# A two-stage attention kernel: block 0 and the scores of block 1 on scaled fp16 parts, the first loads on three queues, and new hand-written orders

## The chip, the core and the metric

The kernel runs on one core of one Trainium2 chip. A core has TensorE (PE, matrix products; its weight loads are shown as PEld), VectorE (DVE), ScalarE (ACT), GpSimd (POOL), SyncE (SP), and 16 DMA engines that serve the queues on which SP, ACT and POOL issue transfers. The metric is the device time of one execution in microseconds (us).

## What is computed

Four images of 256 channels x 1024 points. Block 0 is a group norm, then softmax attention over the points with a residual. Block 1 takes its result x and adds a channel attention and a position attention, both with a residual, which gives 2x + beta * (channel attention) + alpha * (position attention).

```python
def _L0_conv_ref(x, ...):
    h = group_norm(x, gn_w, gn_b)                       # 32 groups
    q, k, v = conv1x1(h, wq, bq), conv1x1(h, wk, bk), conv1x1(h, wv, bv)
    w = softmax(einsum('bcq,bck->bqk', q, k) / sqrt(C))
    return x + conv1x1(einsum('bqk,bck->bcq', w, v), wo, bo)
def _L1_conv_ref(x, ...):
    att = einsum('bcn,bdn->bcd', x, x)                  # 256 x 256
    feat_e = einsum('bcd,bdn->bcn', softmax(max(att) - att), x)
    fb, fc, fd = conv1x1(x, wb, bb), conv1x1(x, wc, bc), conv1x1(x, wd, bd)   # 32, 32, 256 channels
    feat_p = einsum('bcm,bnm->bcn', fd, softmax(einsum('bkn,bkm->bnm', fb, fc)))
    return (beta * feat_e + x) + (alpha * feat_p + x)
```

## The kernel before

**Parts.** Every large product is made from a high and a low part of each operand: `product` (L872 to L875) issues three matmuls, high x high, high x low and low x high. Before the change the parts of block 0 are 32-bit (`f32r`, shown as f32 or fp32r): the weights `a_w` (wq and wk multiplied together) and `b_w` (wv and wo), the normalised input `xn_h` and `xn_l`, and `g_h` and `g_l`. The score operands of block 1, `fb_parts` and `fc_parts`, hold their high and low parts as 96 rows in f32r, so that one matmul makes all three terms. The softmax weights (`pieces`, landed as `land`), V, FD, ET and x1 are already scaled to fp16 parts.

**Steps.** PE works through a hand-written list, `PE_ORDER`; a step has a kind, an image and a number. G.b.c is A times xn for half of the points (12 matmuls of 512 columns), V.b.u is B times xn for four tiles of 128 points (24 matmuls of 256 columns), S0.b.j is one tile of 128 x 1024 scores of block 0 (12 matmuls of 512), S2.b.j the same of block 1 (2 matmuls of 512), O0 and O2 are the weighted sums (each unit x1 is 6 matmuls of 512; O2 has two more units for ET). FBC, FD, ATT, AT and ET belong to block 1. There are 32 S0 tiles, 32 S2 tiles, 8 G and 8 V.

**What follows a tile.** DVE takes its row maximum (max, L690), ACT the exponential (exp, L422), DVE a reciprocal (r, L702 and L704), ACT the high piece (a, L431), DVE the low piece (b, L550), and SP issues a DMA transpose into `land`. Three PSUM buffers hold all score-type results in turn (`SLOTS = 3`): a step that enters a buffer waits until the last user of it is done. `exps` and `pieces` are double. ACT, DVE, POOL and SP have order lists of their own; nothing is reordered at run time, so an instruction that waits holds up all behind it on its engine.

**The start.** SP loads image 0 and then, in its queue, gn_w, gn_b, wo, wv, wd and the small vectors, and then images 1 and 2; ACT loads wk, bq and wq. DVE takes image 0's statistics (bn.0, L726), PE averages them over groups (MEAN.0, VAR.0, L881), POOL makes the inverse root (rstd, L358), DVE the gain and shift (st1) and xn (x0n, L587), ACT its high part (x0h, L408), and DVE or POOL its low part (x0l). PE meanwhile makes bq's bias (BG, L893), the transpose of wo (WO, L900), A and B (L886), the rest of the weights (W) and column sums of absolute weights (SV), from which `fixed_scales` (lS, L612 on) takes the scales of the fp16 parts. G.0.0 and then S0.0.0 are the first large products.

## Time and profile before

| what | us |
|---|---|
| median of three runs (range) | 421.03 (420.3 to 421.5) |
| the profiled execution, its own time | 419.87 |
| the profiled execution, span from first to last instruction | 418.1 |
| PE busy | 399.9 (96%) |
| DVE busy | 307.5 (74%) |
| ACT busy | 240.4 (57%) |
| granted TensorE clock, mean | 0.998 |

The profile page gives the busy time of each engine, the span in 40 slices, and the costliest groups of instructions. A matmul's row gives its start and a modelled duration which overlaps the next one's, so what one matmul costs in a row of them is the distance between starts, not its duration.

### The profile page before, as it was taken

To read this page: it belongs to the slowest core of one execution; us is meant where nothing else is said; L and a number is where in the kernel's file an instruction comes from. 1 tells how busy PE (TensorE), PEld (TensorE's weight loads), DVE (VectorE), ACT (ScalarE), POOL (GpSimd) and SP (SyncE) were. 2 spreads that over 40 slices of the span, in tenths; PEclk is the share of its full clock that TensorE was granted. 3 is DMA by queue.
4 is the path that set the end of the run, shared out by engine and by line. 5 is a ranking of instruction groups with operands and counts; after the bars stand their busy time and mean duration, and the time that the engine had idled before them with its cause. 6 is when DMAs were issued, how large, how long until landed. Compare 5 with 4: busy or idle time off the path is not lost.

```text
span 418.1 us, 5612 instructions
## 1 busy us (share of the span) xinstructions
PE 399.9 (96%) x2012; PEld 253.9 (61%) x2012; DVE 307.5 (74%) x564; ACT 240.4 (57%) x314; POOL 47.5 (11%) x47
## 2 busy tenths in 40 slices
...
GB/s 229 261 45 19 119 114 96 89 68 186 17 100 122 78 88 118 101 120 157 103 88 114 51 102 125 151 102 50 163 140 57 134 88 152 104 195 124 167 192 51
DMA packets 155739, 47.89 MB, mean 115 GB/s; under 512 B 152320, under 2 KB 153664, under 8 KB 155712
## 3 DMA queue, kind: packets, MB, share of 16 engines
...
## 4 chain that ended last, share of the span: by engine, by line
PE 86%; DVE 7%; SPq 2%; issue 2%; DMA 1%; ACT 1%; POOL 0%; DVEq 0%; ACTq 0%
PE sum_ps L873 14%; PE sum_ps L875 14%; PE sum_ps L874 14%; PE score_ps L873 12%; PE score_ps L875 12%; PE score_ps L874 12%; PE score_ps L997 4%; PE score_ps L1018 3%; DVE pieces L550 1%; DMA x<-in_x_dram 1%; DVE bn_raw L726 1%; PE score_ps L1027 1%; DVE x L852 1%; SPq L292 1%; SPq L278 1%
## 5 line engine op out<-in xcount | busy, mean ns | idle before, releaser
L550 DVE SCALAR_TENSOR_TENSOR pieces<-exps,recip,pieces 128x1024 f16<-128x1024 f32 x64 | 88.6, 1388 | 19.9 <-ACT pieces L431 19.5
L431 ACT ACTIVATE pieces<-exps,recip 128x1024 f16<-128x1024 f32 x64 | 72.9, 1143 | 37.6 <-DVE recip L704 27.6
L690 DVE TENSOR_REDUCE negmax<-score_ps 128x1 f32<-128x1024 f32 x64 | 77.4, 1215 | 10.8 <-PE score_ps L997 5.3
L422 ACT ACTIVATE exps<-score_ps,negmax 128x1024 f32<-128x1024 f32 x32 | 35.6, 1112 | 38.1 <-DVE negmax L690 31.7
L873 PE MATMUL score_ps<-xn_h,g_h 128*128 128x512 f32 x128 | 52.8, 412 | 1.1 <-DVE g_l L547 1.1
L422 ACT ACTIVATE exps<-score_ps,negmax_s,scales 128x1024 f32<-128x1024 f32 x32 | 38.4, 1201 | 24.2 <-DVE negmax_s L694 13.8
L875 PE MATMUL score_ps<-xn_h,g_l 128*128 128x512 f32 x128 | 50.1, 391 | 0.0
L874 PE MATMUL score_ps<-xn_l,g_h 128*128 128x512 f32 x128 | 49.9, 390 | 0.0
L873 PE MATMUL sum_ps<-land,fd_h 128*128 128x512 f16 x128 | 48.8, 381 | 0.0
L873 PE MATMUL sum_ps<-land,v_h 128*128 128x512 f16 x128 | 48.7, 381 | 0.0
L874 PE MATMUL sum_ps<-land,fd_h 128*128 128x512 f16 x128 | 48.5, 379 | 0.0
L875 PE MATMUL sum_ps<-land,fd_l 128*128 128x512 f16 x128 | 48.5, 379 | 0.0
L874 PE MATMUL sum_ps<-land,v_h 128*128 128x512 f16 x128 | 48.5, 379 | 0.0
L875 PE MATMUL sum_ps<-land,v_l 128*128 128x512 f16 x128 | 48.5, 379 | 0.0
L378 POOL TENSOR_TENSOR x_parts<-x,x_parts 128x1024 f16<-128x1024 f32 x7 | 15.9, 2272 | 138.3 <-ACT x_parts L395 138.3
L364 POOL TENSOR_TENSOR xn_l<-xn,xn_h 128x1024 fp32r<-128x1024 f32 x6 | 15.5, 2600 | 131.9 <-ACT xn_h L408 87.0
L873 PEld LDWEIGHTS score_ps<-xn_h,g_h 128*128 128x128 f32 x128 | 24.1, 188 | 7.2 <-DVE g_l L547 1.2
L875 PEld LDWEIGHTS score_ps<-xn_h,g_l 128*128 128x128 f32 x128 | 24.0, 188 | 5.3
L874 PEld LDWEIGHTS score_ps<-xn_l,g_h 128*128 128x128 f32 x128 | 24.1, 188 | 4.9
L997 PE MATMUL score_ps<-fc_parts,fb_parts 96*128 96x512 f32 x64 | 24.5, 465 | 0.0
L859 DVE SCALAR_TENSOR_TENSOR x<-sum_ps,scales,x 128x512 f32<-128x512 f32 x16 | 11.3, 745 | 17.2 <-PE sum_ps L875 17.2
L873 PEld LDWEIGHTS sum_ps<-land,fd_h 128*128 128x128 f16 x128 | 12.5, 98 | 17.7 <-issue 5.2
...
## 6 DMA issues: line engine op xcount, KB each, us to landing
...
out_dram<-x POOLq DMA_DIRECT2D x16, 256.0 KB, 3.0
land<-pieces SPq DMA_TRANSPOSE x64, 3.7
x<-in_L_conv_wk_dram ACTq DMA_DIRECT2D x1, 256.0 KB, 4.0
x<-in_L_conv_wq_dram ACTq DMA_DIRECT2D x1, 256.0 KB, 8.0
x<-in_L_conv_wo_dram SPq DMA_DIRECT2D x1, 256.0 KB, 7.8
x<-in_L_conv_wv_dram SPq DMA_DIRECT2D x1, 256.0 KB, 8.0
land<-in_L_conv_wd_dram SPq DMA_DIRECT2D x1, 256.0 KB, 6.4
```

The costliest lines, as they stand in the source:

```text
L364: pool.tensor_tensor(xn_l[:, m, :], xn[:, m, :], xn_h[:, m, :].bitcast(f32), ALU.subtract)\
L378: pool.tensor_tensor(x1_parts[b % 2][:, c, :, 1, :], xs[b][:, :, cols(c, QC)], x1_parts[b % 2][:, c, :, 0, :], ALU.subtract).then_inc(x1_s ...
L422: act.activation(exps[:, n % 2, :], score_ps[s][:, :], ACT.Exp, bias=bias, scale=scale, accum_out=rowsum[:, at]).then_inc(score_done[s], 1)
L431: act.activation(pieces[:, n % 2, 0, :], exps[:, n % 2, :], ACT.Copy, scale=recip[:, n % RING:n % RING + 1]).then_inc(high_piece, 1)
L550: return dve.scalar_tensor_tensor(dst, src, scale, high_part, ALU.mult, ALU.subtract)
L690: last = dve.tensor_reduce(negmax[:, at], ps[:, :], AX.X, ALU.max, negate=True)
L859: dve.scalar_tensor_tensor(part, sum_ps[m][:, :], of_batch(b, OUT_UNIT), part, ALU.mult, ALU.add).then_inc(sum_done[m], 1)
L873: pe.matmul(dst, lhs[0], rhs[0], start=start, stop=False)
L874: pe.matmul(dst, lhs[0], rhs[1], start=False, stop=False)
L875: return pe.matmul(dst, lhs[1], rhs[0], start=False, stop=stop)
L997: last = pe.matmul(ps[:, cols(n, QC)], fb_parts[0:3 * C8, cols(j)], fc_parts[0:3 * C8, cols(n, QC)], start=True, stop=True)
L1018: last = pe.matmul(ps[:, cols(m, QC)].rearrange("p (a k q) -> p a k q", a=2, k=CH), xt[:, c, m, 0, u, :], xt[:, c, :, :, u, :].rearrange(" ...
```

## The change

1. **fp16 parts in block 0 and in the scores of block 1.** `a_w`, `b_w`, `xn_h`, `xn_l`, `g_h`, `g_l`, `fb_parts` and `fc_parts` become fp16. The number and shape of the large products stay.
2. **Scales for them.** A bound of xn comes from gn_w and gn_b (`h_bound`), is maximised over partitions by a small matmul (HX) and made a power of two (`h_scale`, hs), which goes into gn_w and gn_b (U_W, U_B). A bound of G comes from absolute wk and row sums of absolute wq: ACT makes them (wkA, wqA), DVE `r_bound` (rb), PE a product (TG), DVE `g_scales` (gs). A's scale (hA, lA) and G's bias wait for gs. B is copied out of PSUM (cB), its absolute value taken (aB), its column sum added to SV, and it is split (hB, lB) after `fixed_scales`.
3. **Scores of block 0 carry a unit.** The row maximum of an S0 tile is now multiplied by a unit in one more small DVE instruction, as it already was for S2.
4. **Loads.** gn_w, gn_b and bq go on POOL's queue, ahead of the constants that POOL makes; wk, wq, wo, wv on ACT's; SP's starts with image 0 and goes on with wd.
5. **Orders.** All five lists are written anew.

```diff
-        a_w = [sb(f"a_w_{p}", [P, CH, C], f32r) for p in "hl"]
-        b_w = [sb(f"b_w_{p}", [P, CH, C], f32r) for p in "hl"]
+        a_w = [sb(f"a_w_{p}", [P, CH, C], f16) for p in "hl"]
+        b_w = [sb(f"b_w_{p}", [P, CH, C], f16) for p in "hl"]
...
-        xn_h, xn_l = sb("xn_h", [P, CH, N], f32r), sb("xn_l", [P, CH, N], f32r)
-        g_h, g_l = sb("g_h", [P, CH, QC], f32r), sb("g_l", [P, CH, QC], f32r)
+        xn_h, xn_l = sb("xn_h", [P, CH, N], f16), sb("xn_l", [P, CH, N], f16)
+        g_h, g_l = sb("g_h", [P, CH, QC], f16), sb("g_l", [P, CH, QC], f16)
...
-        fb_parts, fc_parts = sb("fb_parts", [P, N], f32r), sb("fc_parts", [P, N], f32r)
+        fb_parts, fc_parts = sb("fb_parts", [P, N], f16), sb("fc_parts", [P, N], f16)
...
-            load_v(GN_W, gn_w, gn_loaded)
-            load_v(GN_B, gn_b, gn_loaded)
-            load_w(wo_sb, wo, wo_loaded)
-            load_w(wv_sb, wv, wv_loaded)
...
         def _(pool):
+            for n, v, loaded in ((GN_W, gn_w, gn_loaded), (GN_B, gn_b, gn_loaded), (BQ, bq, bq_loaded)):
+                with nc.allow_non_contiguous_dma(reason="vectors of 256 words"):
+                    pool.dma_start(vecs[:, n, :], v.rearrange("(m p) -> p m", p=P)).then_inc(loaded, 16)
...
+            for dst, src, loaded in ((wk_sb, wk, wk_loaded), (wq_sb, wq, wq_loaded), (wo_sb, wo, wo_loaded),
+                                     (wv_sb, wv, wv_loaded)):
+                act.dma_start(dst, src.rearrange("(m p) c -> p m c", p=P)).then_inc(loaded, 16)
...
+                if name == "wkA":
+                    act.wait_ge(wk_loaded, 16)
+                    act.activation(abs_w[:, 0:CH, :], wk_sb, ACT.Abs).then_inc(wk_abs, 1)
+                elif name == "wqA":
+                    act.wait_ge(wq_loaded, 16)
+                    for m in range(CH):
+                        last = act.activation(abs_w[:, CH + m, :], wq_sb[:, m, :], ACT.Abs,
+                                              accum_out=vecs[:, WQ_SUM, m:m + 1])
...
             def h_bound():
                 dve.wait_ge(gn_loaded, 32)
...
+                link(dve.tensor_reduce(x_bound[:, 0, 0:1], vecs[:, H_BOUND, :], AX.X, ALU.max))
                 dve.wait_ge(consts_made, 8)
...
+                dve.tensor_scalar(x_diag[:, :], ident[:, :], x_bound[:, 0, 0:1], None, ALU.mult).then_inc(h_diag_made, 1)
...
+            def h_scale():
+                s, ps = wait_full("HX")
+                dve.tensor_reduce(of0(H_MAX), ps[:, 0:P], AX.X, ALU.max).then_inc(score_done[s], 1)
...
+            def g_scales():
...
+                s, ps = wait_full("TG")
+                dve.tensor_reduce(of0(T_MAX), ps[:, 0:C], AX.X, ALU.max).then_inc(score_done[s], 1)
...
-                last = dve.tensor_reduce(negmax[:, at], ps[:, :], AX.X, ALU.max, negate=True)
-                if kind(use) == "S2":
-                    b = numbers(use)[1][0]
-                    link(last)
-                    last = dve.tensor_scalar(negmax_s[:, at], negmax[:, at], of_batch(b, SCORE_UNIT), None, ALU.mult)
-                last.then_inc(score_staged[s], 1)
+                link(dve.tensor_reduce(negmax[:, at], ps[:, :], AX.X, ALU.max, negate=True))
+                dve.tensor_scalar(negmax_s[:, at], negmax[:, at], unit_of(use), None, ALU.mult)\
+                    .then_inc(score_staged[s], 1)
...
 PE_ORDER = """
-    BG MEAN.0 WO VAR.0 A B W MEAN.1 G.0.0 VAR.1 SV S0.0.0 S0.0.1 S0.0.2 S0.0.3 V.0.1 G.0.1 V.0.0 S0.0.4 S0.0.5
+    BG MEAN.0 WO HX VAR.0 A TG W B G.0.0 MEAN.1 SV S0.0.0 S0.0.1 S0.0.2 S0.0.3 G.0.1 V.0.0 VAR.1 S0.0.4 S0.0.5 V.0.1
...
 DVE_ORDER = """
-    bn.0 gb spread.0 gvar.0 st1.0 x0n.0.0 x0n.0.1 bn.1 x0n.1.0 x0l.0.1 lA x0l.0.0 lB x0n.1.1 spread.1 hb gvar.1 cb
+    hb bn.0 gb spread.0 hs gvar.0 rb st1.0 x0n.0.0 x0n.0.1 gs hw x0l.0.0 lA x0l.0.1 bn.1 x0n.1.0 cb x0n.1.1 aB
```

DVE's first rows before the change (L726 bn.0, L743 gb, L565 to L570 spread, L574 gvar):

```order
L726 BN_STATS bn_raw<-x 128x6 x4
L743 TENSOR_SCALAR vecs<-score_ps 128x2
L565 TENSOR_REDUCE stat<-score_ps 128x2
L567 TENSOR_TENSOR diff<-bn_raw,stat 128x8
L569 TENSOR_TENSOR square<-diff 128x8
L570 SCALAR_TENSOR_TENSOR spread_sb<-bn_raw,square 128x8
L574 TENSOR_REDUCE stat<-score_ps 128x2
```

DVE's first rows after it (L610 to L627 hb, L800 bn.0, L823 gb, L584 to L589 spread, L638 the first of hs):

```order
L610 SCALAR_TENSOR_TENSOR x_bound<-vecs 128x2 x2
L623 SCALAR_TENSOR_TENSOR vecs<-x_bound 128x2
L625 TENSOR_REDUCE x_bound<-vecs 128x1
L627 TENSOR_SCALAR x_diag<-ident,x_bound 128x128
L800 BN_STATS bn_raw<-x 128x6 x4
L823 COPY vecs<-score_ps 128x2
L584 TENSOR_REDUCE stat<-score_ps 128x2
L586 TENSOR_TENSOR diff<-bn_raw,stat 128x8
L588 TENSOR_TENSOR square<-diff 128x8
L589 SCALAR_TENSOR_TENSOR spread_sb<-bn_raw,square 128x8
L638 TENSOR_REDUCE block<-score_ps 128x1
```

The bound of xn, which waits for gn_w and gn_b, now stands ahead of image 0's statistics, and hs stands between spread and gvar.

DVE a little later before the change, from image 0's first xn (L587) on, with bn.1 (L726), x0l (L546), lA (L550), lB (L546 and L591):

```order
L587 TENSOR_SCALAR xn<-x,stat 128x512 x2
L726 BN_STATS bn_raw<-x 128x6 x4
L587 TENSOR_SCALAR xn<-x,stat 128x512
L546 TENSOR_TENSOR xn_l<-xn,xn_h 128x512
L550 SCALAR_TENSOR_TENSOR a_w_l<-score_ps,a_w_h 128x512
L546 TENSOR_TENSOR xn_l<-xn,xn_h 128x512
L546 TENSOR_TENSOR b_w_l<-score_ps,b_w_h 128x512
```

And after it, from the last of hw (L680) to aB (L610), with x0l (L565), lA (L569), bn.1 (L800), x0n (L606) and cb (L760):

```order
L680 TENSOR_SCALAR h_wide<-ones,vecs 128x128 x2
L565 TENSOR_TENSOR xn_l<-xn,xn_h 128x512
L569 SCALAR_TENSOR_TENSOR a_w_l<-score_ps,block,a_w_h 128x512
L565 TENSOR_TENSOR xn_l<-xn,xn_h 128x512
L800 BN_STATS bn_raw<-x 128x6 x4
L606 TENSOR_SCALAR xn<-x,stat 128x512
L760 TENSOR_TENSOR vecs<-sum_ps,vecs 128x2
L610 SCALAR_TENSOR_TENSOR vecs<-vecs 128x2
L606 TENSOR_SCALAR xn<-x,stat 128x512
L610 SCALAR_TENSOR_TENSOR abs_w<-e_sb 128x512
```

Image 1's statistics have moved from ahead of G.0.0's inputs (xn's low parts and lA) to behind them.

PE's first rows before the change (L893 BG and bv's product, L881 MEAN and VAR, L900 WO and W, L886 A and B), up to the first large product:

```order
L893 MATMUL score_ps<-vecs,x 128x1 x4
L881 MATMUL score_ps<-bn_raw,group_mean 128x8
L900 MATMUL sum_ps<-ident,x 128x128 x4
L881 MATMUL score_ps<-spread_sb,group_mean 128x8
L886 MATMUL score_ps<-x 128x256 x4
L886 MATMUL score_ps<-land,x 128x256 x4
L900 MATMUL sum_ps<-ident,land 128x128 x4
L920 MATMUL sum_ps<-ident,land 128x32 x6
L893 MATMUL sum_ps<-vecs,land 128x1 x4
L881 MATMUL score_ps<-bn_raw,group_mean 128x8
L873 MATMUL score_ps<-xn_h,a_w_h 128x512
```

And after it (L974 BG, L962 MEAN and VAR, L981 WO and W, L1167 HX, L967 A and B, L1173 TG):

```order
L974 MATMUL score_ps<-vecs,x 128x1 x4
L962 MATMUL score_ps<-bn_raw,group_mean 128x8
L981 MATMUL sum_ps<-ident,x 128x128 x4
L1167 MATMUL score_ps<-x_diag,ones 128x128
L962 MATMUL score_ps<-spread_sb,group_mean 128x8
L967 MATMUL score_ps<-x 128x256 x4
L1173 MATMUL score_ps<-abs_w,h_wide 128x256 x2
L981 MATMUL sum_ps<-ident,land 128x128 x4
L1001 MATMUL sum_ps<-ident,land 128x32 x6
L974 MATMUL sum_ps<-vecs,land 128x1 x4
L967 MATMUL score_ps<-land,x 128x256 x4
L954 MATMUL score_ps<-xn_h,a_w_h 128x512
```

HX and TG are new; B has moved behind W, and MEAN.1 behind G.0.0.

## Rows read from the trace of the kernel before

**Rows 1.** The page: busy time, share, instructions; then the chain that ended last.

```profile
PE 399.9 (96%) x2012; PEld 253.9 (61%) x2012; DVE 307.5 (74%) x564; ACT 240.4 (57%) x314; POOL 47.5 (11%) x47
...
PE 86%; DVE 7%; SPq 2%; issue 2%; DMA 1%; ACT 1%; POOL 0%; DVEq 0%; ACTq 0%
```

**Rows 2.** Windows (us busy per engine), first score tile to last sum.

```profile
28.61:413.24 384.63, 383.68 (x1940) 240.28 (x1940) 289.95 (x520) 232.34 (x302) 40.22 (x29) 1.00 0.51 109
```

**Rows 3.** Timeline of PE (start us, us, what): S0.0.0, V.0.1, G.0.1, V.0.0.

```profile
28.61 0.47 PE L873 MATMUL score_ps<-xn_h,g_h 128*128 128x512 f32 x1 [1.06 <-DVE g_l L547]
...
39.59 0.28 PE L873 MATMUL score_ps<-b_w_h,xn_h 128*128 128x256 f32 x1
...
42.47 0.40 PE L873 MATMUL score_ps<-xn_h,a_w_h 128*128 128x512 f32 x1
...
45.27 0.28 PE L873 MATMUL score_ps<-b_w_h,xn_h 128*128 128x256 f32 x1
```

**Rows 4.** Timeline of PE: FD.0.0 and what follows, then 30 sum matmuls.

```profile
113.38 0.28 PE L873 MATMUL score_ps<-d_w_h,x_parts 128*128 128x256 f16 x1
...
116.01 0.38 PE L873 MATMUL sum_ps<-land,v_h 128*128 128x512 f16 x1
...
334.71 0.39 PE L873 MATMUL sum_ps<-land,v_h 128*128 128x512 f16 x1
...
341.20 0.60 PE L1027 MATMUL score_ps<-ident,e_sb 128*128 128x128 f32 x4
```

**Rows 5.** The chain of waits in time order (start, us): an S2 tile.

```profile
375.84 0.47 PE score_ps L997 x2
```

**Rows 6.** The page: weight loads of f32r and of fp16 parts.

```profile
L873 PEld LDWEIGHTS score_ps<-xn_h,g_h 128*128 128x128 f32 x128 | 24.1, 188 | 7.2 <-DVE g_l L547 1.2
...
L873 PEld LDWEIGHTS sum_ps<-land,fd_h 128*128 128x128 f16 x128 | 12.5, 98 | 17.7 <-issue 5.2
```

**Rows 7.** Timelines of PE and DVE in the start, in order of time.

```profile
4.25 1.29 DVE L726 BATCH_NORM_STATS2 bn_raw<-x 128x6 f32<-128x512 f32 x2 [4.25 <-DMA x<-in_x_dram]
...
7.82 1.84 PE L893 MATMUL score_ps<-vecs,x 128*128 128x1 f32 x8 [7.82 <-DMA vecs<-in_L_conv_bq_dram]
...
9.52 0.57 PE L881 MATMUL score_ps<-bn_raw,group_mean 128*128 128x8 f32 x2
...
10.74 1.12 PE L900 MATMUL sum_ps<-ident,x 128*128 128x128 f32 x4 [0.64 <-DMA x<-in_L_conv_wo_dram]
...
11.94 3.76 PE L886 MATMUL score_ps<-x 128*128 128x256 f32 x8
...
13.91 1.00 DVE L587 TENSOR_SCALAR xn<-x,stat 128x512 f32<-128x512 f32 x2
...
16.95 2.47 DVE L726 BATCH_NORM_STATS2 bn_raw<-x 128x6 f32<-128x512 f32 x4 [2.04 <-DMA x<-in_x_dram]
...
22.20 0.51 PE L873 MATMUL score_ps<-xn_h,a_w_h 128*128 128x512 f32 x1 [1.91 <-DVE xn_l L546]
...
27.06 1.40 DVE L547 SCALAR_TENSOR_TENSOR g_l<-score_ps,vecs,g_h 128x512 fp32r<-128x512 f32 x2
```

**Rows 8.** DMA issues (KB each, median us from issue to landing).

```profile
out_dram<-x POOLq DMA_DIRECT2D x16, 256.0 KB, 3.0
...
vecs<-in_L_conv_gn_b_dram SPq DMA_DIRECT2D x1, 1.0 KB, 7.9
```

**Rows 9.** Groups of instructions of DVE and POOL (busy us, mean ns).

```profile
L550 DVE SCALAR_TENSOR_TENSOR pieces<-exps,recip,pieces 128x1024 f16<-128x1024 f32 x64 | 88.6, 1388 | 19.9 <-ACT pieces L431 19.5
L690 DVE TENSOR_REDUCE negmax<-score_ps 128x1 f32<-128x1024 f32 x64 | 77.4, 1215 | 10.8 <-PE score_ps L997 5.3 <-PE score_ps L875 5.1
...
L704 DVE RECIPROCAL recip<-scaled 128x1 f32<-128x1 f32 x64 | 10.5, 164 | 2.2
...
L694 DVE TENSOR_SCALAR negmax_s<-negmax,scales 128x1 f32<-128x1 f32 x32 | 6.9, 214 | 1.1
...
L371 POOL TENSOR_TENSOR xn_l<-xn,xn_h 128x512 fp32r<-128x512 f32 x2 | 2.9, 1465 | 8.9 <-DVE xn L587 8.9
```

More of the change, by code:

```diff
@@ L15 @@
 HALVES = 3
+PIECES = {"S0": 2.0 ** 15, "S2": 2.0 ** 11}
 PIECE = 2.0 ** 15
```

314 lines of the change are left out of this document (188 added, 126 removed).

## The prediction

> **What bounds the kernel now.** I read the page's busy times and the chain that ended last first: PE is busy for 96% of the span and is 86% of the chain, DVE is second with 74% [rows 1]. Then the window from the first score tile (28.61 us) to the end of the last sum (413.24 us): PE is busy for 383.68 of 384.63 us there, DVE for 289.95, ACT for 232.34, all at the full granted clock [rows 2]. So this kernel is three pieces: a start of 28.6 us in which PE waits for its inputs, 384.6 us in which PE never waits for more than a moment (0.95 us in all), and a tail of 418.1 - 413.2 = 4.9 us, one last addition and store. In the middle only what shortens PE's own stream counts; in the start, only what stands on the chain of first inputs. The profiled execution took 419.87 us, 1.8 above its span, and the median of the runs shown is 1.2 above that. I make the sum on the profiled execution and add 1.2 at the end.
>
> **Part 1, fp16 operands in the middle.** The number of matmuls and their shapes stay, so the question is whether a matmul of 512 columns is issued faster with fp16 than with f32r. The trace has both. Four S0 tiles start at 28.61 and what follows at 39.59: 10.98 / 4 = 2.745 us for a tile of 12, or 229 ns each. V takes 42.47 - 39.59 = 2.88 us for 24 matmuls of 256 columns, G 45.27 - 42.47 = 2.80 us for 12 of 512 [rows 3]. In fp16, 30 sum matmuls of the same shape take 341.20 - 334.71 = 6.49 us, 216.3 ns each, and FD, which has V's shape, takes 116.01 - 113.38 = 2.63 us [rows 4]. An S2 tile takes 0.47 us [rows 5] against 2 x 0.2163 = 0.433. The likely cause is the weight load that comes with each matmul: 188 ns for f32r, 98 for fp16 [rows 6].
>
> - S0: 2.745 - 12 x 0.2163 = 0.15 us, 32 tiles: 4.8 us.
> - V: 2.88 - 2.63 = 0.25, 8 steps: 2.0 us.
> - G: 2.80 - 2.60 = 0.20, the 7 behind the first score tile: 1.4 us.
> - S2: 0.47 - 0.433 = 0.037, 32 tiles: 1.2 us.
>
> Together **9.4 us** off PE's stream. Both ends of each difference are rows of this kernel, so I leave 1 us either way on it.
>
> The Trainium skill speaks against this term. "TensorE: Matmul & The Clock Gate", section "Back-to-back issue gap", gives a warm gap of N/2.4 + 2.5 ns, 216 ns for 512 columns, with no word on the data type. The fp16 rows agree with it and the f32r rows do not; the same page's "Weight-path perf modes" keeps the fast weight load for inputs that are not FP32, which the 188 and 98 ns agree with. By the first rule alone this term would be nothing; that is a rival below.
>
> **Part 2, the small instruction on S0's maxima.** 32 times 214 ns on DVE [rows 9], and some 50 ns of waiting for the maximum: 8.5 us more on DVE. It lies beside PE's work. DVE then has about 290 + 8.5 = 298 busy us in 375, 80% instead of 75%. Queued behind it on DVE are the reciprocals and low pieces of earlier tiles, and ACT's exponential waits for it; PE meets it only when the third PSUM buffer behind is still full. In the first eight tiles cover is thinnest: DVE has `fixed_scales`, lB and image 1's and 2's statistics there as well. I walked PE's and DVE's new lists through these tiles with the durations of rows 9 and found PE waiting some tenths at two or three places, not more. I put 1.5 us of new PE waits on the whole middle, between 0 (as before, where there were 0.95 us in all) and 6 (below).
>
> **Part 3, the new orders in the middle.** They carry the same steps. Where PE now waits for nothing a new order can gain nothing; what it can lose is in the 1.5 us.
>
> **Part 4, the start.** Before, the chain was: DVE's statistics from 4.25; BG, which held PE until bq had landed at 7.8; MEAN.0 at 9.52 to 10.09; xn at 13.91; then DVE stood still until image 1 landed at 16.95, because bn.1 is in front of xn's low parts; G.0.0 at 22.20; lG at 27.06; S0.0.0 at 28.61 [rows 7, 3]. Now:
>
> - hb waits for gn_w and gn_b. When they land on POOL's queue no row shows. Before, gn_b took 7.9 us in SP's queue behind 1 MB of image 0, and landed at 10.1; POOL's stores of 256 KB take 3.0 [rows 8]. Issued at some 1.5 to 2.5 us, that gives 4.5 at the least and 10 at the most. I take 6.0, nearer the low end since nothing big is in this queue. hb is five dependent small instructions at some 0.2: 7.1.
> - Four statistics, 2 x 1.29 [rows 7]: 9.7. BG needs bq, the third in POOL's queue, and takes 1.84; with bq at 7 it is done at 8.9, hidden by DVE. MEAN.0 0.57: 10.3, against 10.09 before.
> - From there to xn were 13.91 - 10.09 = 3.8 us. hs (six dependent levels, 1.3 us) is new on DVE between spread and gvar, as HX is on PE; WO (1.12 us [rows 7]) runs beside spread. rb is new after gvar and waits for ACT's absolute wq, which stands behind WO's copy; POOL's root hides most of it. I add 1.4 in all: xn at 15.5.
> - A cannot start before VAR.0, some 12.3, and takes 3.76 [rows 7]: 16.1. TG 0.5, gs 1.2: 17.8, when lA's scale is ready. hw, x0l, lA, x0l: 0.7 each, with ACT's parts ahead of them: 20.5. B, now behind W, ends about then. **G.0.0 at 20.6**, 1.6 earlier than before, since bn.1 no longer stands in front.
> - DVE then has bn.1 2.47 [rows 7], x0n, cb, x0n 1.3, aB 0.7, spread 0.8, lG 1.40 [rows 7]: 27.2. POOL's two low parts, 1.47 each [rows 9], start at 24.2 and end at the same time. **S0.0.0 at 27.2**, 1.4 us earlier.
>
> wo and wv in ACT's queue and one vector less in front of wq cost nothing here; POOL's constants come some 2 us later, which only BG and hb's last instruction would notice. The Trainium skill, "DMA: Bandwidth & Descriptors", says that queues of SyncE and ScalarE are generally faster than GpSimd's, whose descriptors are written by software; the rows show only that GpSimd's large stores land in 3.0 us, so they do not decide it.
>
> **The sum.** 27.2 + (384.6 - 9.4 + 1.5) + 4.9 = 408.8 us of span, + 1.8 = 410.6 for the execution, against 419.87; with the 1.2 to the median, **411.7 us**.
>
> **Rivals.**
>
> 1. The vectors land late. gn_w, gn_b and bq are 256 pieces of four bytes each, in one queue, beside two busy ones. If gn_b lands at 10 as before, bn.0, MEAN.0 and all behind them move by 4 us, and so does S0.0.0: 411.7 + 4 = 415.7. For it speaks the old 7.9 us; against it that it then stood behind image 0 in the same queue. 13 in 100.
> 2. DVE takes part of the gain back. A tile costs DVE 1.215 + 0.214 + 2 x 0.164 + 1.388 = 3.15 us [rows 9] and PE 2.60. Where four S0 stand in a row PE can be held to DVE's pace; for half a dozen such groups at some 0.8 us the price is 5 us, and the time 415 to 418. Against it: before, 2.9 on DVE met 2.745 on PE and PE did not wait. 9 in 100.
> 3. The same mechanism in full, which ends on the other side: if every S0 tile is held to DVE's pace the price is 32 x 0.55 = 17.6 us. It decides from 0.3 us a tile on, where it eats 9.4 + 1.4 us less the 1.5 already counted; at 0.45 a tile the time is 425. Sums between the tiles, 1.3 us a unit, speak against it. 4 in 100.
> 4. fp16 does not do what it says: the spacing stays at 229 ns because what sets it is not the weight load (the skill's rule without a data type would give this too). Then only the start gains and the 1.5 is lost: 421.1. Rows 4 speak against it, as they have the same shape, engine and PSUM. 4 in 100.
> 5. All goes well: vectors at 4.5 and no new wait: 408.7 or a little under. 4 in 100.
>
> **How the numbers follow.** The forecast, 409 to 414.5, has 66 in 100. The range takes in rivals 1 and part of 2, and goes down by what the vectors and the 1.5 us leave: 408.5 to 417. A difference of 0.3%, about 1.3 us, is what a measurement of this kernel can tell from none. Faster needs all but rivals 3 and 4: 0.92; within 0.3%: 0.04; slower: 0.04.
>
> **What would show it.** In the changed kernel: an S0 tile of 2.60 us from start to start, V 2.63, weight loads of 98 ns on `xn_h`, `g_h`; PE busy over 98% between S0.0.0 and the last sum, in a window of some 377 us; S0.0.0 starting near 27; hb's first row at 6 us, and DVE's first statistics right behind it. It would be wrong if hb starts at 10, if the S0 spacing stays at 229 ns, or if PE shows waits of over 3 us for exponentials (`exps`) or maxima in the middle.

## The result: 415.6 us, 4 us above the forecast

The changed kernel takes 415.62 us (median of 4, 414.8 to 416.5) against 421.26 us for the kernel before: a ratio of 0.987, 95% interval 0.984 to 0.990. It is 1.3% faster, clear of the noise, and lies inside the range of 408.5 to 417, but 3.9 us above the 411.7 forecast and outside the 409 to 414.5 that had 66 in 100. The profiled execution took 414.8 us with a span of 413.0; the sum had 410.6 and 408.8. The difference is in part rival 1, the late vectors, and in part two things in the start that stood nowhere in the prediction. Its 415.7 us and the measured 415.6 meet by chance: the vectors landed at 9, not at 10, and being late explains 2.6 us of the difference, not 4.

The page of the changed kernel, busy time first, then the chain that ended last, the weight loads of the scores, and two DMA issues:

```profile
PE 390.5 (95%) x2018; PEld 203.9 (49%) x2018; DVE 311.5 (75%) x620; ACT 245.3 (59%) x320; POOL 49.1 (12%) x50
...
PE 88%; DVE 5%; DMA 4%; issue 1%; POOL 1%; SPq 0%; POOLq 0%; DVEq 0%
...
L954 PEld LDWEIGHTS score_ps<-xn_h,g_h 128*128 128x128 f16 x128 | 12.6, 99 | 17.7 <-DVE g_l L566 3.0
...
land<-pieces SPq DMA_TRANSPOSE x64, 4.3
...
vecs<-in_L_conv_gn_b_dram POOLq DMA_DIRECT2D x1, 1.0 KB, 6.7
```

Windows of the changed kernel (busy us of PE, PEld, DVE, ACT, POOL, then granted clock, DMA share, GB/s): from the first score tile to the end of the last sum, and its first 3.6 us alone.

```profile
30.41:408.31 377.90, 375.56 (x1942) 191.83 (x1942) 291.35 (x558) 235.92 (x303) 40.33 (x30) 1.00 0.59 111
...
30.41:34.00 3.59, 3.59 (x10) 1.30 (x11) 3.34 (x27) 0.05 (x1) 0.00 (x0) 0.55 0.02 5
```

Set against [rows 2]: the start ends at 30.41 us instead of 28.61 (forecast 27.2), the middle is 377.9 long instead of 384.6 (forecast 376.7), the tail 413.0 - 408.3 = 4.7 (forecast 4.9). So the whole gain is the middle's, 6.7 us, and the start gives 1.8 back.

The start of the changed kernel, all engines in order of time (start us, us, engine, what; the idle time ahead of it and what ended it). It answers to [rows 7] and to the S0.0.0 row of [rows 3]:

```profile
2.21 0.74 POOL L348 DMA_DIRECT2D vecs<-in_L_conv_gn_b_dram  x1
...
8.98 0.23 DVE L610 SCALAR_TENSOR_TENSOR x_bound<-vecs 128x2 f32<-128x2 f32 x2 [8.98 <-DMA vecs<-in_L_conv_gn_b_dram]
...
9.83 2.47 DVE L800 BATCH_NORM_STATS2 bn_raw<-x 128x6 f32<-128x512 f32 x4
...
10.32 1.84 PE L974 MATMUL score_ps<-vecs,x 128*128 128x1 f32 x8 [10.32 <-DMA vecs<-in_L_conv_bq_dram]
...
14.40 3.04 PE L967 MATMUL score_ps<-x 128*128 128x256 f32 x8
...
17.65 1.00 DVE L606 TENSOR_SCALAR xn<-x,stat 128x512 f32<-128x512 f32 x2
...
22.49 0.39 PE L954 MATMUL score_ps<-xn_h,a_w_h 128*128 128x512 f16 x1 [1.07 <-DVE xn_l L565]
...
26.06 2.65 POOL L384 TENSOR_TENSOR xn_l<-xn,xn_h 128x512 f16<-128x512 f32 x2 [9.04 <-DVE xn L606]
26.50 0.16 DVE L584 TENSOR_REDUCE stat<-score_ps 128x2 f32<-128x8 f32 x1
26.70 0.93 DVE L586 TENSOR_TENSOR diff<-bn_raw,stat 128x8 f32<-128x8 f32 x1
27.66 1.08 DVE L588 TENSOR_TENSOR square<-diff 128x8 f32<-128x8 f32 x1
28.77 0.17 DVE L589 SCALAR_TENSOR_TENSOR spread_sb<-bn_raw,square 128x8 f32<-128x8 f32 x1
28.86 1.40 DVE L566 SCALAR_TENSOR_TENSOR g_l<-score_ps,vecs,g_h 128x512 f16<-128x512 f32 x2
...
30.41 0.58 PE L954 MATMUL score_ps<-xn_h,g_h 128*128 128x512 f16 x1 [2.39 <-DVE g_l L566]
30.79 0.63 PE L955 MATMUL score_ps<-xn_l,g_h 128*128 128x512 f16 x1
```

Read it downwards. gn_b is issued on POOL's queue at 2.21 and is there at 8.98; hb stands first on DVE, so bn.0 starts at 9.83, though image 0 was there early (its halves had landed by 4.4 and 6.7 us in the kernel `mean_first` below, which loads it in the same way). xn follows at 17.65 (forecast 15.5), G.0.0 at 22.49 (20.6). Then come two things nobody had on the list. While POOL makes its two low parts, 26.06 to 28.71, two DVE instructions on eight columns take 0.93 and 1.08 us instead of 0.17; they belong to spread.1, which nobody waits for yet, but lG stands behind them, and S0.0.0 waits for lG. The price of such a meeting could be read in the trace of the kernel before, where the same `diff` ran beside POOL's subtraction and took as long as that:

```profile
23.88 1.28 POOL L371 TENSOR_TENSOR xn_l<-xn,xn_h 128x512 fp32r<-128x512 f32 x1 [2.29 <-DVE xn L587]
23.91 1.28 DVE L567 TENSOR_TENSOR diff<-bn_raw,stat 128x8 f32<-128x8 f32 x1
```

And the first matmuls of S0.0.0 stand 0.38 to 0.43 us apart instead of 0.216: the granted clock was 0.55 of full, mostly the lower level of 1.2 GHz, for 3.6 us, right after PE had been idle for 2.39 us.

In the middle PE waits for more than before. Its waits in the changed kernel (us in total, times, longest):

```profile
PE score_ps L954 <- DVE g_l L566: 2.4, 1, 2.4
PE sum_ps L954 <- DMA land<-pieces: 1.8, 2, 1.2
...
PE sum_ps L954 <- DVE x L940: 0.4, 1, 0.4
PE score_ps L1102 <- issue: 0.2, 1, 0.2
```

Behind S0.0.0 these are 1.8 + 0.4 + 0.2 = 2.3 us (rounded from the rows; 377.90 - 375.56 gives 2.34). The sum had about as much, the 0.95 us of before and 1.5 new ones, but for other reasons: 1.8 of the 2.3 are transposed pieces that had not landed. In the changed kernel they take 4.3 us from issue to landing. In the kernel before it was this:

```profile
land<-pieces SPq DMA_TRANSPOSE x64, 3.7
```

The diff leaves these transfers as they are and moves only the XD steps among them in SP's list. What it does change is where they lie: the new small tensors and the fp16 tensors ahead of them move `exps`, `pieces` and `land` in SBUF from a multiple of 512 bytes (land at 175616) to 416 bytes past one (161696). These addresses are not in the traces; they are the sizes of the kernel's tensors added up, each rounded up to 32 bytes.

### The profile page after: what moved, and what is told of

Its sections match the earlier page's. It is cut to its first block, busy times and chain, and to the rows that moved or that the text cites. A ratio compares the mean times of both kernels' runs of the same rounds, so it can differ in the third digit from the quotient of the medians.

```text
span 413.0 us, 5690 instructions
## 1 busy us (share of the span) xinstructions
PE 390.5 (95%) x2018; PEld 203.9 (49%) x2018; DVE 311.5 (75%) x620; ACT 245.3 (59%) x320; POOL 49.1 (12%) x50
## 4 chain that ended last, share of the span: by engine, by line
PE 88%; DVE 5%; DMA 4%; issue 1%; POOL 1%; SPq 0%; POOLq 0%; DVEq 0%
PE sum_ps L954 15%; PE sum_ps L955 15%; PE sum_ps L956 15%; PE score_ps L954 12%; PE score_ps L955 12%; PE score_ps L956 12%; PE score_ps L1102 3%; PE score_ps L1081 3%; DMA land<-pieces 3%; DMA vecs<-in_L_conv_gn_b_dram 2%; DVE bn_raw L800 1%; PE score_ps L1111 1%; DVE pieces L569 1%; DVE xn L606 0%; PE score_ps L962 0%
## 5 line engine op out<-in xcount | busy, mean ns | idle before, releaser
L569 DVE SCALAR_TENSOR_TENSOR pieces<-exps,recip,pieces 128x1024 f16<-128x1024 f32 x64 | 85.3, 1337 | 19.5 <-ACT pieces L439 19.3
L430 ACT ACTIVATE exps<-score_ps,negmax_s,block 128x1024 f32<-128x1024 f32 x32 | 38.4, 1200 | 29.9 <-DVE negmax_s L768 23.5
L954 PE MATMUL score_ps<-xn_h,g_h 128*128 128x512 f16 x128 | 49.2, 384 | 2.4 <-DVE g_l L566 2.4
L955 PE MATMUL score_ps<-xn_l,g_h 128*128 128x512 f16 x128 | 49.2, 384 | 0.0
L956 PE MATMUL score_ps<-xn_h,g_l 128*128 128x512 f16 x128 | 49.0, 383 | 0.0
L377 POOL TENSOR_TENSOR xn_l<-xn,xn_h 128x1024 f16<-128x1024 f32 x6 | 12.8, 2134 | 80.4 <-ACT xn_h L420 80.4
L954 PEld LDWEIGHTS score_ps<-xn_h,g_h 128*128 128x128 f16 x128 | 12.6, 99 | 17.7 <-DVE g_l L566 3.0
L956 PEld LDWEIGHTS score_ps<-xn_h,g_l 128*128 128x128 f16 x128 | 12.7, 99 | 15.6 <-issue 0.8
L954 PEld LDWEIGHTS sum_ps<-land,v_h 128*128 128x128 f16 x128 | 12.6, 98 | 15.8 <-issue 2.0
L956 PEld LDWEIGHTS sum_ps<-land,fd_l 128*128 128x128 f16 x128 | 12.5, 98 | 15.1
```

Source lines behind the costliest of these rows:

```text
L377: pool.tensor_tensor(xn_l[:, m, :], xn[:, m, :], xn_h[:, m, :], ALU.subtract)\
L430: act.activation(exps[:, n % 2, :], score_ps[s][:, :], ACT.Exp, bias=negmax_s[:, at], scale=unit_of(use), accum_out=rowsum[:, at]).then_in ...
L569: return dve.scalar_tensor_tensor(dst, src, scale, high_part, ALU.mult, ALU.subtract)
L954: pe.matmul(dst, lhs[0], rhs[0], start=start, stop=False)
L955: pe.matmul(dst, lhs[0], rhs[1], start=False, stop=False)
L956: return pe.matmul(dst, lhs[1], rhs[0], start=False, stop=stop)
```

## Experiments

Three questions: is the gain of the middle really the data type's; what are the three losses (late vectors, the lower clock, slower transposes) worth each, and what causes them; and how far does a kernel get without them. Every time is stated against the kernel before, run beside it on the same chip; there its median was 421.4 to 422.2. The changed kernel itself was not run again beside them; 0.987 of the median beside f32r_back, aligned, lg_first and warm, 421.98, is 416.5.

The spans compared below are those of one profiled execution each, and the 413.0 of the changed kernel belongs to the fastest of its four. By the ratios (0.987 against 0.980, 0.980 and 0.979) `aligned`, `lg_first` and `warm` gain about 3 us each, by the spans 2.0, 2.8 and 1.9. The intervals, 0.3% to either side, leave room for both, so the gains that follow are good to about 1 us.

### f32r_back: the data type alone

```diff
-        a_w = [sb(f"a_w_{p}", [P, CH, C], f16) for p in "hl"]
+        a_w = [sb(f"a_w_{p}", [P, CH, C], f32r) for p in "hl"]
...
-        fb_parts, fc_parts = sb("fb_parts", [P, N], f16), sb("fc_parts", [P, N], f16)
+        fb_parts, fc_parts = sb("fb_parts", [P, N], f32r), sb("fc_parts", [P, N], f32r)
```

(b_w, xn_h, xn_l, g_h, g_l likewise; the bounds' operands share fb_parts and fc_parts again so that all fits.)

> The changed kernel with the operands of G, V, S0 and S2 (a_w, b_w, xn_h, xn_l, g_h, g_l, fb_parts, fc_parts) in f32r again; scales, orders, start and every instruction stay. Theory (the data type alone shortens the spacing): S0 tiles go from 2.60 back to 2.74 us, V to 2.88, G to 2.80, S2 to 0.47, weight loads to 188 ns, and the middle is 32 x 0.145 + 8 x 0.25 + 7 x 0.20 + 32 x 0.037 = 9.2 us longer: about 425 us. Rival (the gain came from the new order and fewer waits, and the spacing does not hang on the type): within 1 us of the changed kernel's 415.6. A third outcome, that a longer PE stream swallows the waits of 2.3 us that the changed kernel has in the middle, would give 7 to 8 us.

Measured: 422.99 us, ratio 1.004 (1.002 to 1.006). The scaled kernel without fp16 is no faster than the kernel before. Window of the middle, then the weight loads of the scores (busy us, mean ns):

```profile
30.73:415.85 385.12, 384.76 (x1942) 240.90 (x1942) 293.25 (x558) 236.50 (x303) 41.67 (x30) 1.00 0.57 108
...
L956 PEld LDWEIGHTS score_ps<-xn_h,g_h 128*128 128x128 f32 x128 | 24.3, 190 | 8.9 <-DVE g_l L568 3.2 <-DVE fd_l L571 0.3
```

The middle is 385.12 - 377.90 = 7.2 us longer, and the span 7.6. PE's waits there fall from 2.3 to 0.4 us, and the lower clock costs 1.7 us at its head (0.60 of full for 4.3 us) where it cost 1.6 (0.55 for 3.6), so PE's own stream is 383.1 us against 374.0 and grew by 9.1, where 9.2 was expected. The weight loads are at 190 ns again. Theory confirmed, with the third outcome: with the slower PE the waits for landed pieces are gone, though they still land in 4.3 us, and 1.9 us come back. That the weight load is the way by which the type acts is not shown: both operands of each matmul changed their type together.

### aligned, pad32, pad224: where pieces and land lie

```diff
+        pad = sb("pad", [P, 24])
         exps = sb("exps", [P, 2, N])
```

> The changed kernel with an unused tensor of 96 bytes a partition ahead of exps, so that exps, pieces and land start at a multiple of 512 bytes again, as they do in the kernel before; now they start at 416 past one. Nothing else moves. Theory (the transposing DMAs are slower because source and destination are off a 64-byte line): landing falls from a median of 4.3 to 3.7 us, ACT's wait for landed pieces from 15.6 to about 10 us, PE's largest wait (1.24 us at 62.4) goes, and the time falls by 1 to 1.7 us to about 414.3. Rival (they land later because PE's faster stream packs the same transfers closer together): landing stays at 4.2 to 4.3 and the time at 415.6.

Measured: 412.81 us, ratio 0.980 (0.977 to 0.983), against 0.987. The span falls from 413.0 to 411.0. Of aligned, landing and the window of the middle:

```profile
land<-pieces SPq DMA_TRANSPOSE x64, 3.7
...
30.32:406.27 375.95, 375.13 (x1942) 192.10 (x1942) 291.28 (x558) 235.96 (x303) 40.31 (x30) 1.00 0.52 111
```

Landing is back at 3.7 us, PE waits for no landed piece any more, and the middle is 375.95 us, 1.95 shorter. One number of the expectation was wrong: ACT's wait for landed pieces stayed at 15.5 us. It was never the costly one. Nor did nothing else move, as the expectation has it: the small tensors behind `land` moved by 96 bytes too. But landing goes with the address in all fourteen kernels of this study: 3.7 us in the six where `pieces` and `land` start at a multiple of 512, 4.3 us in the eight where they don't.

Two more kernels ask which boundary counts, with 8 and 56 words in place of 24.

> The changed kernel with an unused tensor of 32 bytes a partition ahead of exps: exps, pieces and land then start at a multiple of 64 bytes (448 past a multiple of 512) instead of 32 past one. In the run before, 96 bytes brought them to a multiple of 512 and the landing of the transposes from 4.3 to 3.7 us. Theory (64 bytes is what counts): landing 3.7 us and a span of about 411, like the 411.0 with 96 bytes. Rival (the page of 512 counts): landing stays 4.3 us and the span at 413.

> The changed kernel with 224 bytes ahead of exps: exps, pieces and land start 128 past a multiple of 512. So far: 0 past it gave 3.7 us of landing, 448 past it (a multiple of 64) 4.3, 416 and 160 past it 4.3. Theory (a multiple of 128 is enough): 3.7 us and a span near 411. Rival (256 or 512 is needed): 4.3 us and a span near 413.

Measured, one execution each: spans of 413.9 and 414.5 us. The landings, of pad32 and then of pad224:

```profile
land<-pieces SPq DMA_TRANSPOSE x64, 4.3
```

```profile
land<-pieces SPq DMA_TRANSPOSE x64, 4.3
```

So 448 and 128 past a multiple of 512 are as slow as 416 and 160 (f32r_back, also 4.3); only 0 is fast. Both theories of a smaller boundary fall. 256 was not tried. The Trainium skill, "DMA: Bandwidth & Descriptors", section "How a descriptor splits into AXI transactions", says that a transaction has to start at a 256-byte boundary and that a descriptor that doesn't pays for bytes it does not use. The five offsets agree with that rule, and it would make 256 a fast one; no run here shows it.

### lg_first and warm: DVE's detour and the lower clock

```diff
-... x0n.1.1 aB spread.1 lG.0.0 lS
+... x0n.1.1 aB lG.0.0 spread.1 lS
```

> The changed kernel with one pair of steps exchanged on DVE: lG.0.0 (the low part of the first G, for which S0.0.0 waits) ahead of spread.1 (image 1's statistics, whose second and third instruction took 0.93 and 1.08 us beside POOL's low parts instead of 0.17). Theory (S0.0.0's last wait is that detour): lG starts at about 26.6 and ends at 28.0, S0.0.0 starts when POOL's second low part ends, at 28.7, 1.6 to 1.7 us earlier than 30.4; PE's pause before it shrinks from 2.4 to 0.8 us, and if it is the pause that lowers the granted clock, the 1.7 us at the lower clock go too: 415.6 - 3.3 = 412.3 us. Rival A (the clock falls all the same): 413.9. Rival B (POOL slows lG in its turn, as it slowed the two small instructions): lG takes 2 to 3 us and S0.0.0 gains at most 0.7: 415.

Measured: 412.0 us, ratio 0.980 (0.976 to 0.983), a span of 410.2. Of lg_first, DVE and PE in order of time, and the window of the middle:

```profile
26.66 1.41 DVE L566 SCALAR_TENSOR_TENSOR g_l<-score_ps,vecs,g_h 128x512 f16<-128x512 f32 x2
27.98 0.16 DVE L584 TENSOR_REDUCE stat<-score_ps 128x2 f32<-128x8 f32 x1
28.18 0.63 DVE L586 TENSOR_TENSOR diff<-bn_raw,stat 128x8 f32<-128x8 f32 x1
...
29.03 0.38 PE L954 MATMUL score_ps<-xn_h,g_h 128*128 128x512 f16 x1 [0.95 <-POOL xn_l L384]
...
29.03:405.47 376.44, 373.92 (x1942) 191.65 (x1942) 291.58 (x559) 235.84 (x303) 40.33 (x30) 1.00 0.59 111
```

lG keeps its 1.4 us beside POOL (rival B falls), S0.0.0 starts 1.4 us earlier, PE's pause is 0.95 us, and the clock stays up in this execution. In four of the other five the mean granted clock was 0.989 to 0.996, so it does not stay up always. POOL's second low part ends at 28.78; the one instruction on eight columns that still overlaps it takes 0.63. The slow ones read two tensors from SBUF; lG and the sum at 27.98 read PSUM and keep their length. The Trainium skill, "SBUF — State Buffer", section "SBUF: two separate sides", states this as a rule: an instruction of VectorE with two SBUF inputs and one of GpSimd hold one pair of ports exclusively, each for its whole length. The trace agrees: `diff` ends at 27.63 and `square` at 28.74 in the changed kernel, near the ends of POOL's two instructions (2.65 us for both from 26.06), and in the kernel before `diff` and the subtraction last 1.28 us each from 23.9. By overlap alone it is argued, not isolated; no run moved POOL's work.

```diff
+                keep_busy(5)        # ones x ident into columns 112 to 240 of the second bank of SV's buffer
                 pe.wait_ge(h_bound_made, 1)
...
-                last.then_inc(score_full[s], 1)
+                keep_busy(8).then_inc(score_full[s], 1)
```

> The changed kernel with 13 extra matmuls of 128 columns into columns of a score buffer that nothing reads, 5 ahead of SV's (in PE's pause of 1.5 us) and 8 behind them (in the pause of 2.4 us before S0.0.0). Theory (the granted clock falls to 0.5 for 3.4 us because PE was idle before S0.0.0): the clock stays at 1.0, the first S0 matmuls are 216 ns apart instead of 430, S0.0.0 starts at 30.4 as now, and the time falls by 1.7 us to 413.9. Rival (the dip has another cause, or the idle time before 22 us carries over): the dip stays and the time is 415.6 or, if SV is held up, up to 0.5 above.

Measured: 412.42 us, ratio 0.979 (0.976 to 0.983), a span of 411.1. Of warm, the first matmul of S0.0.0 and the window of its first 3.6 us:

```profile
30.32 0.38 PE L954 MATMUL score_ps<-xn_h,g_h 128*128 128x512 f16 x1 [0.73 <-DVE g_l L566]
...
30.30:33.90 3.60, 3.58 (x17) 1.68 (x18) 3.39 (x28) 0.03 (x1) 0.00 (x0) 1.00 0.02 5
```

S0.0.0 starts where it did, the clock is 1.00, and the middle is 376.0 us, 1.9 shorter. Work whose result nobody reads, in PE's pauses, is worth 1.9 us by the spans: the clock stayed up, as the theory says. The median came out 1.5 us below the 413.9 that it gave. The four executions of the changed kernel had a mean clock of 0.992 to 0.995, warm's six have 0.997 or more, so in most of them more was repaired than the one dip that the theory reckoned with.

### vec_hw and mean_first: the late vectors

```diff
+            for n, v in ((GN_W, gn_w), (GN_B, gn_b)):      # on SP, ahead of image 0
+                load_v(n, v, gn_loaded)
...
-            for n, v, loaded in ((GN_W, gn_w, gn_loaded), (GN_B, gn_b, gn_loaded), (BQ, bq, bq_loaded)):   # on POOL
```

(bq goes to the head of ACT's queue.)

> The changed kernel with gn_w and gn_b at the head of SP's queue ahead of image 0, and bq at the head of ACT's ahead of wk, instead of three loads in POOL's queue; orders stay. Theory (POOL's queue takes 6.7 us for 1 KB because it is POOL's, and three issues of 0.8 us hold up its constants): the vectors land by about 4 us, hb starts there, bn.0 follows as soon as image 0 is there (about 5), 4 us earlier than now; A, TG and all behind them follow as far as wq and wo are there, S0.0.0 near 27 and the time near 412. Rival (256 pieces of four bytes are slow in any queue and hold up the big loads behind them, as gn_b took 7.9 us behind image 0 in the kernel before): gn_b lands at 6 or later, image 0 and wq land 2 us later than now, and S0.0.0 gains at most 1 us: 414.6 or above.

Measured: 413.0 us, ratio 0.979 (0.974 to 0.985), a span of 410.7. Of vec_hw, the landing of gn_b, then DVE and PE:

```profile
vecs<-in_L_conv_gn_b_dram SPq DMA_DIRECT2D x1, 1.0 KB, 3.2
...
4.59 0.23 DVE L611 SCALAR_TENSOR_TENSOR x_bound<-vecs 128x2 f32<-128x2 f32 x2 [4.59 <-DMA vecs<-in_L_conv_gn_b_dram]
...
7.24 1.29 DVE L801 BATCH_NORM_STATS2 bn_raw<-x 128x6 f32<-128x512 f32 x2 [1.71 <-DMA x<-in_x_dram]
...
28.85 0.38 PE L955 MATMUL score_ps<-xn_h,g_h 128*128 128x512 f16 x1 [2.40 <-DVE g_l L567]
```

Both sides were half right. At the head of SP's queue the same 1 KB lands in 3.2 us instead of 6.7 on POOL's, but image 0, now third in that queue, lets bn.0 start at 7.24 instead of the 4.36 of the next kernel. S0.0.0 gains 1.6 us, not 3.4. Whether POOL's queue itself is slow is not shown: here the vectors were issued at 0.80 and 1.33 us, ahead of every large load, and in the changed kernel at 1.34 and 2.21, behind the first loads of image 0 and wk. PE's pause ahead of S0.0.0 is 2.40 us again, and so is the dip: the granted clock was 0.50 from 30 to 32 us.

The other way is to leave the loads and let nothing wait for them that needn't:

```diff
-    BG MEAN.0 WO HX VAR.0 A TG W B G.0.0 MEAN.1 SV S0.0.0 S0.0.1 ...       # PE
+    MEAN.0 VAR.0 HX BG WO A TG W G.0.0 B MEAN.1 S0.0.0 SV S0.0.1 ...
...
-    hb bn.0 gb spread.0 hs gvar.0 rb st1.0 x0n.0.0 x0n.0.1 gs hw x0l.0.0 lA x0l.0.1 bn.1 ...   # DVE
+    bn.0 spread.0 hb gvar.0 hs rb st1.0 gb x0n.0.0 x0n.0.1 x0l.0.0 x0l.0.1 gs hw lA x0n.1.0 ...
```

> The changed kernel with its start in another order, so that nothing but what needs them waits for the vectors. DVE: bn.0 and spread.0 ahead of hb, low parts of the first half ahead of gs, bn.1 behind x0n, lG.0.0 ahead of spread.1. PE: MEAN.0, VAR.0 and HX ahead of BG, W ahead of G.0.0, B and SV behind it. Theory (the vectors that land at 9 us hold up the statistics, and with them the whole start): bn.0 starts near 4.3 and ends at 6.8, hb runs from 9.0, HX at 9.9, A at about 12.4 to 15.4, lA ends near 18.7, G.0.0 starts near 19 (22.5 now) and S0.0.0 near 24.5 (30.4 now). With the lower clock gone too that gives 415.6 - 5.9 - 1.7 = 408 us; if the clock falls again while PE waits for lG, 409.7. Rival (PE's own work at the lower clock and the landing of bq at 10.3 bound the start, or the small DVE instructions now meet POOL's low parts): S0.0.0 not before 27, 412 or above.

Measured: 413.05 us, ratio 0.979 (0.975 to 0.983), a span of 410.8. Of mean_first, DVE and PE in order of time:

```profile
4.36 1.29 DVE L800 BATCH_NORM_STATS2 bn_raw<-x 128x6 f32<-128x512 f32 x2 [4.36 <-DMA x<-in_x_dram]
6.66 1.29 DVE L800 BATCH_NORM_STATS2 bn_raw<-x 128x6 f32<-128x512 f32 x2 [1.01 <-DMA x<-in_x_dram]
...
13.42 3.62 PE L967 MATMUL score_ps<-x 128*128 128x256 f32 x8
...
20.54 0.38 PE L954 MATMUL score_ps<-xn_h,a_w_h 128*128 128x512 f16 x1 [1.03 <-issue]
...
21.33 0.63 PE L954 MATMUL score_ps<-xn_h,a_w_h 128*128 128x512 f16 x1
...
27.87 0.38 PE L954 MATMUL score_ps<-xn_h,g_h 128*128 128x512 f16 x1 [1.05 <-DVE g_l L566]
```

The statistics start at 4.36 as expected, but S0.0.0 only reaches 27.87, not 24.5. A starts 1.0 us later than thought, behind BG and WO, and takes 3.6; gs stands behind the low parts; and this time the lower clock catches G.0.0, whose matmuls stand 0.43 us apart from 21.33 on (granted clock 0.56 from 20.54 to 24.40). Of the 5.9 us hoped for 2.5 came: the rival that PE's own work bounds the start was nearer. It stands at 413, no better than the much smaller lg_first.

One thing this and the next expectations read into the trace: that PE is at the lower clock before 20 us. The granted clock is given as 1.00 there, in every kernel. What speaks for a lower one is only the lengths: A takes 3.04 us in the changed kernel and 3.62 here, while B, matmuls of the same number and shape, takes 1.97 and 1.89 later on.

### lg_aligned, start_cold, start_warm, start_tuned: putting it together

> Both earlier edits together: lG.0.0 ahead of spread.1, and the 96 bytes ahead of exps. If the two repairs are independent their gains add: lG first alone gave a span of 410.2 and alignment alone 411.0, against 413.0, so 2.8 + 2.0 = 4.8 off: span 408.2, about 410 us. If the waits for landed pieces and the start hide each other (an earlier start only meets the next wait sooner), no more than the better of the two: 412.

Measured: 409.38 us, ratio 0.972 (0.968 to 0.975), a span of 407.6 where adding both gains gave 408.2. They are independent.

start_cold is mean_first with the 96 bytes and with gs ahead of the low parts:

```diff
-... x0n.0.1 x0l.0.0 x0l.0.1 gs hw lA x0n.1.0 ...
+... x0n.0.1 gs x0l.0.0 x0l.0.1 lA hw x0n.1.0 ...
```

> The start in the order of mean_first, with gs ahead of the low parts on DVE, and the 96 bytes ahead of exps. In mean_first the granted clock was low until 20.5 us and again for the first G, from 21.0 to 24.4. Theory (alignment is worth the same 2.0 us of span here, and gs 1.4 us earlier brings A's scale and G.0.0 about 1 us forward): S0.0.0 near 26.9, span 410.8 - 2.0 - 1.0 = 407.8, about 410. Rival (waits move into the middle, where SV's matmuls and the scales behind them now stand after S0.0.0): 411 or above.

Measured: 411.27 us, ratio 0.974 (0.971 to 0.978), but a profiled execution of 409.2 with a span of 407.5. S0.0.0 starts at 25.68. By the median the rival's 411 is met, by the profiled execution the theory's 410; the table below shows why the two differ. start_warm adds matmuls that nobody reads:

```diff
+            fill = {"MEAN.0": 10, "VAR.0": 4, "G.0.0": 4, "S0.0.0": 5}
...
+                keep_busy(fill.get(step, 0))
```

> start_cold plus 23 matmuls of 128 columns whose result nothing reads, in four pauses of PE: 10 ahead of MEAN.0, 4 ahead of VAR.0, 4 ahead of G.0.0, 5 ahead of S0.0.0. Theory (PE's pauses are what keeps the clock low in the start and lets it fall at G.0.0): the clock is at 1.0 from about 10 us on, A takes 1.9 us instead of 3.1 to 3.6, G 2.6 instead of 4.2, and S0.0.0 starts 3 us earlier than in start_cold, near 24: 3 us less, about 407. Rival (the start is bound by DVE's chain of small instructions, not by PE): A and G are faster but S0.0.0 moves by less than 1.5 us, 408.5 or above.

Measured: 409.25 us, ratio 0.971 (0.968 to 0.974), a span of 407.5, the same as start_cold's, though the median is 2.0 us lower: four of its six executions ran at 409.2, two of start_cold's did. Of start_warm, PE:

```profile
5.78 4.64 PE L1150 MATMUL score_ps<-ident,ones 128*128 128x128 f32 x20 [5.78 <-POOL bbc_bias L365]
...
13.96 1.89 PE L968 MATMUL score_ps<-x 128*128 128x256 f32 x8
...
25.81 0.38 PE L955 MATMUL score_ps<-xn_h,g_h 128*128 128x512 f16 x1
...
PE score_ps L955 <- ACT exps L431: 1.3, 2, 1.2
```

A takes 1.89 us, so by its length the clock did rise. But the ten matmuls take 4.64 us, 0.46 each where five of the same kind take 1.36 us later (0.27 each), and hold up MEAN.0 from 7.9 to 10.2; the two cancel. And in both kernels PE waits for exponentials soon after, since they stand behind lS and hB. The last kernel repairs both:

```diff
-            fill = {"MEAN.0": 10, "VAR.0": 4, "G.0.0": 4, "S0.0.0": 5}
+            fill = {"MEAN.0": 4, "VAR.0": 1, "G.0.0": 5, "S0.0.0": 4}
...
-... max0.0.0 r0.0.0 lS max0.0.1 ...
+... max0.0.0 lS r0.0.0 max0.0.1 ...
-... exp0.0.0 a0.0.0 hB exp0.0.1 ...
+... exp0.0.0 hB a0.0.0 exp0.0.1 ...
```

> start_warm with fewer matmuls whose result nothing reads (4 ahead of MEAN.0 instead of 10, 1 instead of 4 ahead of VAR.0, 5 instead of 4 ahead of G.0.0, 4 instead of 5 ahead of S0.0.0), and lS directly behind the first maximum on DVE, hB directly behind the first exponential on ACT. In start_warm ten of them held MEAN.0 up until 10.2 us, where its input was there at 7.9, and PE waited 1.86 us for exponentials between 38 and 45 us, since they stood behind lS and hB. Theory (both are this arrangement's own mistakes): MEAN.0 at about 8.0, A 1.9 us long from about 12.4, G.0.0 at 18.3, S0.0.0 at about 24 instead of 25.8, the waits at 38 to 45 us under 0.5: span 407.5 - 1.8 - 1.4 = 404.3, about 406 us. Rival (four matmuls do not raise the clock, so A takes 3 us and S0.0.0 stays at 25.7): 407.7 if only the waits go, 409 if they don't.

Measured: 408.01 us, ratio 0.970 (0.966 to 0.973), a span of 406.5. Of start_tuned, PE:

```profile
13.02 3.62 PE L968 MATMUL score_ps<-x 128*128 128x256 f32 x8
...
26.20 0.38 PE L955 MATMUL score_ps<-xn_h,g_h 128*128 128x512 f16 x1
...
PE score_ps L963 <- ACT exps L431: 0.5, 1, 0.5
```

The rival holds for the start: with four of them ahead of MEAN.0, A takes 3.62 us again, and S0.0.0 starts at 26.20. The waits for exponentials went (1.9 to 0.5 us), and that is what it gains. It has the lowest ratio of the study, 13.4 us below the kernel before beside it; its interval and those of start_warm and lg_aligned overlap.

### What the executions say of the clock

Each execution comes with its mean granted clock. Beside it stands its time:

| kernel | clock | us |
|---|---|---|
| start_cold | 1.000 (2 executions) | 409.07, 409.22 |
| start_cold | 0.996 (4) | 411.16 to 411.85 |
| lg_aligned | 0.997 to 0.999 (4) | 409.18 to 409.42 |
| lg_aligned | 0.994 (2) | 410.91, 411.22 |
| warm | 0.997 to 1.000 (6) | 412.27 to 412.78 |
| start_tuned | 0.998 to 1.000 (6) | 407.32 to 408.75 |
| kernel before, beside lg_aligned | 0.998 (2) | 419.04, 419.39 |
| kernel before, beside lg_aligned | 0.985 to 0.990 (9) | 421.44 to 424.08 |

In start_cold, lg_aligned and the kernel before, the same program meets the lower clock in some executions and not in others, and that goes with some 2 us of time. The mean clock does not always tell the time, though: lg_first took 411.96 us at 0.999 and 411.93 at 0.993, and start_tuned's two executions at 1.000 are slower (408.21, 408.65) than its two at 0.998 (407.48, 407.32). The profiled execution of the kernel before was one at 0.998, and of the eleven in the table only two are. That is the likely cause of the 1.2 us between profile and median that the prediction carried along without one. The two kernels whose pauses are filled, and whose clock did not fall in the profile, kept it at 0.997 or above in all twelve executions; start_warm, which has a pause of 1.2 us left at 38 us, did not in two of six (0.996, 410.5 and 410.7).

## The prediction, point by point

**What bounds the kernel**: right. PE is busy for 375.6 of 377.9 us in the middle, the start and the tail are what is left.

**Part 1, 9.4 us off PE's stream**: right, in mechanism and in size. S0's matmuls stand 0.216 us apart, weight loads take 99 ns against the 188 of [rows 6]. Undoing the type alone gives 9.1 us; the middle without waits and without the lower clock, 377.9 - 2.3 - 1.6 = 374.0, is 9.7 below the 384.63 - 0.95 of before. The 0.6 us between these two figures stay unexplained, and that the weight load is the cause stays the likely reading that the prediction called it. The rule without a data type, rival 4, gave 421.1 and is out: f32r_back measured 423.0 where the same kernel in fp16 stands at 416.5.

**Part 2, DVE**: the 32 small instructions came (6.9 us), but DVE's busy time in the middle went only from 289.95 to 291.35 us, not to 298; 3.3 us of the difference are the 64 low pieces, which took 1337 ns each instead of the 1388 of [rows 9]. Rivals 2 and 3 are out: none of PE's waits in the middle is for a maximum or an exponential.

**New waits, 1.5 us**: the size was met by luck. Waits went from 0.95 to 2.34 us, so 1.4 are new, but 1.8 of the 2.3 are for landed pieces, which the prediction looked at nowhere; the cause of the slower landing is the address, as `aligned` shows. Whether PE has to wait for it depends on the rest: vec_hw and f32r_back, where pieces land in 4.3 us too, show no such wait.

**Part 4, the start, S0.0.0 at 27.2**: 30.41, the term that failed. Its first step, "I take 6.0, nearer the low end since nothing big is in this queue", took the size of what is in the queue for what sets the latency; the vectors took 6.7 us and landed at 8.98. The bounds were 4.5 to 10, so the landing came near rival 1 (at 10, 415.7 us), to which I had given 13 in 100; by its own rule a landing at 9 makes 414.7, and the rest of the 415.6 is what follows here. The steps behind it were sized well: from the end of bn.0 (12.3) to the xn steps 5.3 us passed, where the sum had 5.8 from 9.7, and from there to G.0.0 4.8 against 5.1. From G.0.0 to S0.0.0 it was 7.9 us against 6.6: lG stood behind a spread.1 that the sum gave 0.8 us without asking what POOL does beside it; it took 2.4 (26.50 to 28.94), and in the kernel before the same step had taken 1.9 (23.72 to 25.59) for the same reason. Late statistics 2.6, these parts -0.5, -0.3 and +1.3: that is the 3.2 us. The lower clock in the first S0 tile, 1.6 us behind that, has no term at all: the sum took the middle's matmuls at full clock because [rows 2] shows 1.00, and did not ask what a longer pause of PE ahead of S0.0.0 (2.39 us, 1.06 before [rows 3]) would do.

**To add up**: start +3.2, middle +1.2 (clock +1.6, waits 2.34 against 0.95 + 1.5, so -0.1, and the stream 374.0 against 383.7 - 9.4 = 374.3, so -0.3), tail -0.2 make the 4.2 us between 408.8 and 413.0. That the vectors were late is worth 1.6 us by vec_hw's repair and more by the sum; the detour with the pause behind it 2.8 (lg_first), the address 2.0 (aligned). Of these only the address lies outside what the diff says it does; the place of spread.1 is part of the new orders.
